# Queries and keys in DRAM: dims outermost with their two parts adjacent, and four stores of 128 rows by two chunks per batch in place of eight

## What is computed

```python
xn = layernorm(x)
# attention: 16 heads of 16 dims; row i sees rows i-128 .. i
q, k, v = xn @ Wq.T + bq, xn @ Wk.T + bk, xn @ Wv.T + bv
attn = softmax(where(mask, q @ k.T * 0.25, -10000)) + 1e-9
a = (attn @ v) @ Wo.T + bo
# experts: 8 of 256 x 512, two chosen per row, and one shared
f = sum over the chosen e of sigmoid(logit_e) * (silu(xn @ gate_e) * (xn @ up_e)) @ down_e
f = f + (silu(xn @ sh_gate) * (xn @ sh_up)) @ sh_down
out = x + a + f
```

## Time and profile before

| | |
|---|---|
| median of 3 runs | 2066.87 us (2055.52 to 2069.42) |
| the profiled execution | 2073.88 us, its span 2071.9 us |
| TensorE busy, matmul / weight load | 1728.1 us (83%) / 1421.9 us (69%) |
| VectorE, ScalarE, GpSimd busy | 1129.1 us (54%), 905.9 us (44%), 808.9 us (39%) |
| moved by DMA | 333.80 MB, 161 GB/s on average |
| granted TensorE clock, mean | 0.902 of full speed |

### The profile page before, as it was taken

How to read it: one execution, slowest core, us unless ns; L and a number is a source line. 1 busy time by engine, 2 the same in 40 slices (tenths; PEclk the granted TensorE clock), 3 DMA queues, 4 the chain that set the end, 5 groups by cost and what they waited for, 6 DMA issues and landing times.

```text
span 2071.9 us, 38865 instructions
## 1 busy us (share of the span) xinstructions
PE 1728.1 (83%) x11609; PEld 1421.9 (69%) x11610; DVE 1129.1 (54%) x3465; ACT 905.9 (44%) x1737; POOL 808.9 (39%) x757
## 2 busy tenths in 40 slices
PE   6936545550999999999999988889899999899987
PEld 6925535540888888888888865666666666666666
DVE  6653232331666666666666665565565655555552
ACT  2312111111555554545455435555555655555553
POOL 0024332340000000000000026788788888888886
PEclk9998777775999999999999968899888998998998
DMA  8447766765444444444444447666677767777752
GB/s 281 141 146 220 226 208 203 221 212 191 148 147 147 145 149 151 152 152 152 152 152 152 129 102 146 145 161 154 146 157 153 166 158 160 152 160 154 155 125 75
DMA packets 254491, 333.80 MB, mean 161 GB/s; under 512 B 26992, under 2 KB 172656, under 8 KB 252400
## 3 DMA queue, kind: packets, MB, share of 16 engines
q1 hardware_dynamic: 202368, 261.44, 46.3%
q0 software_dynamic: 12288, 33.57, 6.5%
q10 hardware_dynamic: 39792, 38.28, 5.5%
HBM read 210.52 MB, written 112.72 MB: 156 GB/s over the span
## 4 chain that ended last, share of the span: by engine, by line
PE 54%; SPq 14%; issue 12%; DMA 10%; POOL 4%; ACT 3%; DVE 2%; another core or an unknown queue 0%; ACTq 0%; POOLq 0%; DVEq 0%
PE psum L148 31%; PE psum L783 11%; SPq L576 7%; DMA plain_arena<-xn_d 4%; DMA split_arena<-k_d 4%; PE psum L1227 4%; PE psum L1267 2%; PE psum L1250 2%; SPq L811 2%; PE psum L854 2%; SPq L813 2%; ACT plain_arena L1369 1%; POOL split_arena L1169 1%; POOL plain_arena L1152 1%; DMA plain_arena<-y_d,b_ix 1%
## 5 line engine op out<-in xcount | busy, mean ns | idle before, releaser
L148 PE MATMUL psum<-split_arena 128*128 128x512 f32 (+1 forms) x4560 | 996.0, 374 | 20.4 <-POOL split_arena L1169 10.8
L148 PEld LDWEIGHTS psum<-split_arena 128*128 128x128 f32 x4560 | 787.4, 201 | 159.3 <-POOL split_arena L1169 17.0
L1462 DVE CUSTOM_DVE_ANT_0 plain_arena<-psum,mask 128x256 f32<-128x256 f32 (+1 forms) x1024 | 340.2, 386 | 306.0 <-PE psum L1227 276.8
L1369 ACT ACTIVATE plain_arena<-psum 128x512 f32<-128x512 f32 (+1 forms) x512 | 250.8, 543 | 322.4 <-PE psum L1250 282.9
L1212 POOL MEMSET plain_arena<- 128x256 f32 x1 | 0.3, 312 | 699.0 <-ACTq L137 699.0
L783 PE MATMUL psum<-split_arena 128*128 128x256 f32 x1872 | 233.8, 285 | 0.0
L1227 PE MATMUL psum<-split_arena 48*128 48x256 f32 (+1 forms) x1024 | 169.8, 356 | 70.1 <-DMA split_arena<-k_d 44.9
L783 PEld LDWEIGHTS psum<-split_arena 128*128 128x128 f32 x1872 | 226.9, 192 | 0.1
L1227 PEld LDWEIGHTS psum<-split_arena 48*128 48x128 f32 x1024 | 106.1, 205 | 149.3 <-issue 71.8
L613 POOL DMA_INDIRECT sorted_d<-plain_arena,q_idx x128 | 124.2, 970 | 206.1 <-DVE q_idx L700 170.4
L900 ACT ACTIVATE plain_arena<-psum 128x512 f32<-128x512 f32 x156 | 93.3, 598 | 219.3 <-PE psum L148 219.1
(11 more groups left out here) (132 smaller groups left out, 1946.7 us busy)
## 6 DMA issues: line engine op xcount, KB each, us to landing
plain_arena<-in_gate_w SPq DMA_DIRECT2D x39, 512.0 KB, 5.1
plain_arena<-in_up_w SPq DMA_DIRECT2D x39, 512.0 KB, 6.2
plain_arena<-in_down_w SPq DMA_DIRECT2D x39, 512.0 KB, 7.0
plain_arena<-sorted_d SPq DMA_DIRECT2D x39, 512.0 KB, 3.9
y_d<-plain_arena ACTq DMA_DIRECT2D x39, 512.0 KB, 3.6
plain_arena<-in_x SPq DMA_DIRECT2D x32, 512.0 KB, 3.9
plain_arena<-xn_d SPq DMA_DIRECT2D x32, 512.0 KB
q_d<-split_arena SPq DMA_DIRECT2D x64, 256.0 KB
```

The source lines that it names most:

```text
L148: last = pe.matmul(out, lhs_t(p), rhs(q), start=(begins and c == 0 and k == 0), stop=(ends and c == len(chunks) - 1 and k == 2), skip_grou ...
L1369: act.activation(b_pt[:, g % 2, 2 * p + par, 4 * half:4 * half + n, :].rearrange("p k s -> p (k s)"), psum[:, 2 + par, 0:n * P], ACT.Exp, ...
L1462: last = dve.tensor_tensor_reduce(b_junk[:, 2 * par + i % 2, 0:cols], psum[:, par, at:at + cols], mask[:, 2 * P - cols:2 * P], -1.0, 3e38, ...
```

## The change

Queries and keys are laid out (batch, column, part, row) in DRAM, where a column is head x 16 + dim, so that the two parts of one dim are neighbours, 2 KB each. For queries the high part is first, for keys the low part. A store takes one part of all 256 columns of a batch: 128 partitions by two chunks of 128 columns, 512 KB. There are four per batch in place of eight. The loads of attention read the same bytes into 48 partitions again, with both the lone part at the first 16 and the pairs (two parts of dim 0, two of dim 1, ...) at the 32 behind them. The semaphore counts follow the number of stores.

```diff
-    q_d = nc.dram_tensor("q_d", (B, H, 2, DH, S), F32).ap()
-    k_d = nc.dram_tensor("k_d", (B, H, 2, DH, S), F32).ap()
+    q_d = nc.dram_tensor("q_d", (B, D, 2, S), F32).ap()
+    k_d = nc.dram_tensor("k_d", (B, D, 2, S), F32).ap()
...
                 for k, dram in enumerate((q_d, k_d)):
                     for part in range(2):
-                        for m in range(KD):
-                            sp.dma_start(dram[ds(b, 1), m * 2 * HG:(m + 1) * 2 * HG, part, :, :].rearrange(
-                                "o h d s -> (o h) d s"), q_qk[:, u, k, part, m, :].bitcast(F32)).then_inc(q_st[u], 16)
+                        sp.dma_start(dram[ds(b, 1), :, part if k == 0 else 1 - part, :].rearrange(
+                            "o (m p) s -> p (o m) s", p=P), q_qk[:, u, k, part, :, :].bitcast(F32)).then_inc(q_st[u], 16)
...
-                sp.sem_inc(q_st[u], 128)
+                sp.sem_inc(q_st[u], 64)
...
-                sp.wait_ge(q_st[u], 128 * (B // 2) + 128)
+                sp.wait_ge(q_st[u], 64 * (B // 2) + 64)
...
-                act.wait_ge(q_st[u], 128 * n + 128)
+                act.wait_ge(q_st[u], 64 * n + 64)
...
-                for dram, tile, once, both in ((q_d, b_q, 0, 16), (k_d, b_k, 32, 0)):
-                    heads = dram[ds(b, 1), g * HG:(g + 1) * HG, :, :, :].rearrange(
-                        "o (p q) w d s -> q (o w d) p s", q=2)[par]
-                    sp.dma_start(tile[at + once:at + once + 16, g, :, :].bitcast(F32), heads[0:DH]
-                                 ).then_inc(b_ldqk[g], 16)
-                    sp.dma_start(tile[at + both:at + both + 32, g, :, :].bitcast(F32), heads
+                for k, (dram, tile) in enumerate(((q_d, b_q), (k_d, b_k))):
+                    rows = dram[ds(b, 1), g * 64:(g + 1) * 64, :, :].rearrange(
+                        "o (p q d) w s -> q (o d) w p s", q=2, d=DH)[par]
+                    sp.dma_start(tile[at:at + 16, g, :, :].bitcast(F32), rows[:, k, :, :]).then_inc(b_ldqk[g], 16)
+                    sp.dma_start(tile[at + 16:at + 48, g, :, :].bitcast(F32), rows.rearrange("d w p s -> (d w) p s")
                                  ).then_inc(b_ldqk[g], 16)
```

## The result

| | before | changed | ratio |
|---|---|---|---|
| median of 4 runs, first chip | 2062.47 us | 1939.94 us (1931.73 to 1948.97) | 0.9407 (0.935 to 0.9464) |
| the profiled execution | 2073.88 us | 1937.82 us | |
| its span | 2071.9 us | 1935.8 us | |

The change takes 122.5 us off, 5.9%.

A forecast was written before the change was run, and what follows sets the result against it. One half of the DMA engines, 98% busy, was taken to bound the projection stage. Its 235 us of work, spread evenly at share 0.95, gives 247 us instead of 349: 2066.87 - 102 = 1965 us, range 1947 to 2007.

The forecast's parts named there:

- Part 1: Projection stage: stores of 128 rows by two chunks use 16 engines; stage 247 us instead of 349, 102 us gained.
- My factor of 0.95 for gaps: Projection stage: assumed DMA share after the change, turning 235 us of work into a stage of 247 us.
- Part 2: Projection stage: TensorE, GpSimd, ScalarE and the `xn_d` loop all stay within 15.4 us per batch, so DMA still bounds.
- the loop through `xn_d`: Projection stage: load, transposes, values, bias, `v_d` store, next load; about 28 us of 30.8 available per two batches.
- Part 3: SP queue, projection stage: half as many store issues; nothing added to the gain.
- Part 4: DRAM layout: attention's reads cost nothing, 5 us either way; store rows 4 KB apart cost nothing.
- Part 5: Matmuls of the scores: the same three products in another order over 48 rows, costing nothing.
- Rival A: Projection stage: stores writing 4 KB apart move more slowly; 1999 to 2022 us (7%), or slower, 2102 us (3%).
- f = 1.47: Projection stage stores: slowdown factor if held to the skill page's 207 GB/s instead of 304; 2018 us.
- Rival B: Projection stage: another loop takes over at about 18 us per batch; gain 61 us, 2006 us; chance 8%.
- C: Projection stage: TensorE stays at its lower clock, 21 us per batch, stage 336 us, 2054 us; chance 2%.
- D: Projection stage: new stores still run on 8 engines, or SBUF is the limit; time stays 2067 us; chance 3%.

The follow-up runs named there:

- h2: The kernel of h1 with 2 KB left empty behind each head in DRAM; 2058.7 us, ratio 1.0019 to the kernel before.
- h1: The changed kernel with eight stores of 256 KB per batch again, in the new layout; 1922.2 us, ratio 0.9364 to the kernel before.
- h3: The kernel before with each store cut in two, of 4 heads and 64 partitions each; 2163.9 us, ratio 1.0521.
- h5: The changed kernel, unaltered, run again on another chip than the first; 1918.0 us, ratio 0.9347 to the kernel before.
- k2: The changed kernel with the parts outermost in DRAM, so that stores write rows 2 KB apart; 1944.7 us, ratio 0.9440 to the kernel before.
- k and n runs: Seven runs on two chips, of the changed kernel unaltered or with edits to stores, layout or line 635; 1928.7 to 1945.8 us.
- m runs: Three runs on one chip: the changed kernel, with line 635 later, and with that plus rows of 4 KB; 1915.8, 1916.4 and 1906.7 us.
- m3: The changed kernel with line 635 after the keys' matmuls and stores in rows of 4 KB; 1906.7 us, ratio 0.9286 to the kernel before.

## Why the prediction was right in kind and wrong in size

*The reading of the bound* was right: one half of the DMA engines bound the stage. h2 shows it with nothing but a gap in DRAM added to h1, and h3, with the stores on four engines, makes it worse.

*Part 1, sixteen engines for the new stores,* was right: 16.3 completions per store. *Its size was wrong, and this is the step that failed:* "The work of the stage is 0.673 x 349 = 235 us of all 16 engines", with 235 us as the least that the stage could take. It is neither. Spread over sixteen engines the same 72.7 MB took 0.91 x 228 = 207 us of all engines' time on the first chip and 205 us at share 1.00 in h5. I took the busy share as a fixed amount of work, but the same packets took less time once they were spread: per packet of the hardware queue it was 0.512 x 349 x 16 / 26048 = 110 ns before and 0.763 x 205 x 16 / 26048 = 96 ns in h5. The least that the stage could take should have come from bytes over the best rate on record: stage one's tail had shown 400 GB/s, which gives 182 us, too short for a forecast but a true lower end. At h5's 355 GB/s, which no row of before showed, the stage takes 205 us. My factor of 0.95 for gaps was near on the first chip (a share of 0.91) and moved the sum further off on the prompt ones (1.00).

*Part 2, "None is above 15.4 us, so DMA still bounds the stage",* holds on chips with prompt signals and fails on the first, the chip of the result, where its list of waits has none for a store. There a loop of 14.5 us per batch is last: values on TensorE, bias and sum on VectorE, line 635 on TensorE. I summed engines' busy times and the loop through `xn_d`, but not this one. It would have been under 15.4 us, so my wrong DMA term hid the omission; the 12.8 us per batch that h5 shows would have made every loop near 14 us worth adding up. The two errors work against each other on the first chip: DMA was priced too dear and the loop was left out. That the forecast missed the gain by 20 us there (122.5 for 102) and not by the 33 of h5's chip is in part luck.

*Part 3* (fewer issues are worth nothing by themselves) was right: h1. *Part 4* (the reads of attention, the 4 KB pitch, at nothing) was right as far as the spread of 18 us behind the stage can tell; loads of `k_d` in attention did not land later (5.1 us in the first profile and 5.6 in h5, 6.4 before), and k2 shows the same engine time per byte for the 4 KB pitch. *Part 5* was right: the expert stage did not move, and attention by no more than its spread.

*Rival A* fell with k2 and h2. The estimate of 2018 us from the Trainium skill ("DMA: Bandwidth & Descriptors", section Latency and other measured facts) did not come true either; the stage moved 319 GB/s, with 33.6 of its 72.8 MB in these stores. The page's pitch is the one from partition to partition, and its list begins at 512 KiB; here the rows of neighbouring partitions lie 4 KB apart and only the two chunks of a store 512 KB, so no run tests it and it is not to be read down to 4 KB. The page also gives 214 GB/s as the full rate of the same copies, so that its 207 at 512 KiB is hardly a loss, and f = 1.47 was no fair price to draw from it. *Rival B,* another loop takes over, was the right idea with the wrong loop and the wrong size: it takes over at 14.5 us, not at 18. *C and D* did not occur; the granted clock rose from 0.73 to 0.85, as the shorter idles had suggested. The range ended at 235 us for the stage, and so at 1947 us: it missed because its lower end rested on the term that failed and had nothing for that term being too high.

## What to carry to other kernels

Count the completion packets of a DMA before believing a mean DMA share: a share of 0.67 was, by the forecast's estimate, half of the engines at 0.98, and an outermost dimension of 8 in DRAM that could not be merged with the next was all there was to it. Take the lower end of a range from bytes at the best rate that the trace shows for any stretch, not from the busy share of the crowded stretch, and then add up every loop between engines against the new, shorter period, since the next one may be only 2 us away. Before taking a profile for the kernel's nature, profile it on a second chip.

## What the runs showed of the hardware beyond that

- TensorE's signals reach VectorE 2 to 5 us late, in bunches, on some chips and not on others (the first chip and those of the k and n runs against those of the h2 to h5 and m runs), in a stage that is otherwise the same. The changed kernel's stage took 228 to 231 us with them and 205 to 206 without; the stages of before and h2, bound by their stores, took 349.9 with and 349.1 without. They were late in the projection and the attention stage and not in the expert stage.
- Per loaded engine the stores and the rest moved at 19.0 GB/s with the stores on 8 engines, and at 23.4 and 22.1 with them on 4 and 16 (33.55 and 39.2 MB shared out as above). Packets of 2 KB took 102 ns on average on 8 engines, 88 on 4 and 87 on 16, with a median of 84 each time.
- Sixteen engines sustained 355 GB/s for 205 us of mixed stores, loads and scatters, and 368 GB/s with rows of 4 KB (m3).
